# Expert results weighted on leaving PSUM and added by the scatter into two sums per token

## The chip, the cores and the metric

The kernel runs on one core of one Trainium2 chip. The metric is device time in microseconds (us) of one launch. The kernel before takes 664.97 us, the median of three runs (664.3 to 666.75).

## The reference, cut to what matters

A layer of 2048 tokens by 256 features: a retention block with its own MLP, then a mixture of experts. The change touches the second half alone, from the expert outputs to the sum over experts. All arithmetic is float32.

```python
x = hidden_states.reshape(-1, H)                      # 2048 x 256
routing_probs = softmax(x @ gate_w.T)                 # 16 experts
topk_w, topk_idx = top_k(routing_probs, 4)
topk_w = topk_w / topk_w.sum(-1)
combine = (one_hot(topk_idx, 16) * topk_w[..., None]).sum(1)
shared = silu_mul(x @ shared_gate_up.T) @ shared_down.T * sigmoid(x @ shared_gate_vec.T)
for each expert e:
    h = silu_mul(x @ w_gu[e].T)                       # 176 hidden features
    sparse += (h @ w_d[e].T) * combine[:, e]
out = x_in + gb * (shared + sparse)
```

## The kernel before, in words

One program per engine, ordered by hand-placed semaphores; nothing is planned by costs. Two blocks follow each other with a barrier between them.

**First block.** Retention over 16 tiles of 128 tokens, then the first MLP over 4 groups of 512 tokens. SP (the DMA-issuing engine) works down one list. After the retention loads it issues 20 DMAs at L1077 that fill the DRAM table `dispatched` (80 tiles of 128 rows, 260 floats a row) from a zeroed tile `fill`; column 256 of each such row holds a spare destination number. Then SP waits for the last tile of retention (`x2_lo`), and only behind that wait do the loads of the shared expert's weights (L1066) and the next `x` tiles stand.

**Second block, shared stage.** The shared expert's MLP runs over 4 groups g of 6 blocks b. VectorE (DVE) carries between its blocks the routing work, placed by `route(g, b)`: `bases` and `slots(k)` (where each token's k-th choice goes in `dispatched`), `less_best` (logits minus their maximum), `weigh(k)` (the exponential of the k-th choice, by L1661 and L1662), `share` (the normalized weights). ScalarE (ACT) takes the exponentials (L1554, L1555) in block g = 0, b = 5, between two Silu activations. GpSimd (POOL) writes the destination number of the k-th choice (token x 4 + k) into column 256 of the token rows (`number`, L1527) and scatters the rows into `dispatched`, 64 indirect DMAs (L1542), paced by the gate products of TensorE (PE).

**Second block, expert stage.** 80 tiles of 128 dispatched rows, each of one expert. SP loads a tile into one of 16 buffers `xe` (L1869); PE transposes it (L2009), multiplies by the gate and up weights (L2025), transposes the hidden features (L2035) and multiplies by the down weights (L2043, L2045); ACT and DVE split each operand into a high and a low part. `result` on DVE (L1972) multiplies the PSUM result by the vector `gb` into one of 4 buffers `yb`, and `send` on POOL (L1893) scatters the 128 rows by an indirect DMA to the DRAM table `results`, one row per token and choice. `alone` is an instruction that does nothing, ahead of each scatter. `send(j)` waits for `y` of tile j only. `result(j)` waits until the scatter of tile j - 4 has landed, and the load of tile j until that of tile j - 16 has.

**Second block, last stage.** When all 80 scatters have landed, SP loads for each of 16 token tiles its four rows per token (L1884, 512 KB each). DVE forms `acc = ys[k] * weights[k] + acc` for k = 0 to 3, starting from the residual rows, tiles in pairs: 64 operations (L1990). ACT issues the store of a finished tile (L1940).

Of the kernel before, what the change touches and what calls it, by code (L numbers as in the profile page):

```python
# [16 lines left out]
ALU = mybir.AluOpType  # L17
# [3 lines left out]
P = 128  # L21
N = 2048
# [30 lines left out]
def shape_tables():  # L53
# [27 lines left out]
        "t_tiles": np.ascontiguousarray(np.broadcast_to(np.arange(ETILES, dtype=f32)[None], (P, ETILES))),  # L81
        "t_dest": ((np.arange(NT)[None, None, :] * P + s[:, None, None]) * TOPK + np.arange(TOPK)[None, :, None]).astype(np.int32),
        "t_spare": (SPARE + np.arange(4)[None, :] * P + s[:, None]).astype(np.int32),
    }
# [27 lines left out]
def mlp_buffers(sb):  # L112

    b1, b2 = sb("b1", [P, FB]), sb("b2", [P, E])
    wr = sb("wr", [P, KB, NR])
    xt, res = sb("xt2", [P, TPG, E]), sb("res", [P, TPG, E])
    stats = sb("m_st6", [P, 2, 6]), sb("m_mv", [P, 2, 2]), sb("m_ve", [P, 2, 1]), sb("m_rstd", [P, 2, 1])
    xn, hT32 = sb("m_xn", [P, 2, E]), sb("hT32", [P, 2, KB, P])
    fill, spare = sb("fill", [P, 4, ROW]), sb("spare", [P, 4], mybir.dt.int32)
    return b1, b2, wr, xt, res, stats, xn, hT32, fill, spare  # L120


def build(nc, io, out):
    ctx = ExitStack()
    dram = {n: nc.dram_tensor(n, shape, F32, kind="Internal").ap() for n, shape in (
        ("dispatched", (ETILES * P, ROW)), ("results", (N * TOPK + 4 * P, E)), ("x3_rows", (N, E)), ("x4_rows", (N, E)))}
    with ctx:
# [895 lines left out]
def mlp(nc, io, sem, wait, alone, bank, ident, neghalf, modb, h_all, x2T, wf1, wf2, act1, a1, near, early, h3T,  # L1023
# [9 lines left out]
    stage = rows[:, STAGE:NT, :].rearrange("p t c -> p (t c)")[:, 0:2 * KB * GU].rearrange("p (c k n) -> p c k n", c=2, k=KB)  # L1033
    names = """st_in0 st_in1 w_hi w_lo zeros spare_in fill gab xb b1in b2in wr_in x_in0 x_in1 x_in2 x_in3 res1 res f_ps act a_hi a_lo fc2 x3
        st6 mv ve rstd xn h3 tr_ps h32 hi lo lg_ps lg versus ahead order chosen start before
# [16 lines left out]
    def sync(sp):  # L1052
# [41 lines left out]
        for i in range(TPG):  # L1094
            store(NT - TPG + i, i)
        sp.wait_ge(s_filled, 16 * (ETILES // 4))
        sp.wait_ge(S["x3_out"], 16 * NT)
        for i in range(TPG):
            sp.wait_ge(S[f"row_out{i}"], 16 * NG)

    def load_spare():
        nc.sync.dma_start(spare[:, :], io["t_spare"]).then_inc(S["spare_in"], 16)

    def empty_rows():
        pool = nc.gpsimd
        nc.gpsimd.memset(fill[:, :, :], 0.0).then_inc(S["zeros"], 1)
        pool.wait_ge(S["zeros"], 1)
        pool.wait_ge(S["spare_in"], 16)
        nc.gpsimd.tensor_copy(fill[:, :, E:E + 1].bitcast(mybir.dt.int32), spare[:, :].unsqueeze(2)).then_inc(S["fill"], 1)

# [291 lines left out]
def shared_and_dispatch(nc, io, sb, sem, wait, alone, bank, gb, weights, tile_expert, h3T, rows, logits,  # L1402
# [16 lines left out]
    steps, tile_no = sb("steps", [P, NX]), sb("tile_no", [P, ETILES])  # L1419
    dest = sb("dest", [P, TOPK, NT], INT)  # L1420
    best = sb("best", [P, NT])
# [5 lines left out]
    ecount = sb("ecount", [1, ETILES])  # L1427
    wsum, wrec = sb("wsum", [P, NT]), sb("wrec", [P, NT])
    names = """tab_in ones st_in0 st_in1 w_hi w_lo z_ps g_ps u_ps act hid a_hi a_lo fc2 x_in0 x_in1 x_in2 x_in3 sh x4 x4_out0 x4_out1 x4_out2 x4_out3
# [84 lines left out]
    def gpsimd(pool):  # L1514
        nc.gpsimd.memset(rows[:, :, E:ROW], 0.0).then_inc(S["pad"], 1)
        nc.gpsimd.memset(ones[:, :], 1.0).then_inc(S["ones"], 1)
# [30 lines left out]
    def scalar(act):  # L1547
# [39 lines left out]
    def vector(dve):  # L1587
# [71 lines left out]
        def weigh(k):  # L1659

            chain(nc.vector.scalar_tensor_tensor(flat(pick), flat(order), float(k), flat(ez), ALU.is_equal, ALU.mult))  # L1661
            chain(nc.vector.tensor_reduce(weights[:, k, :], pick[:, :, :], AX.X, ALU.add))  # L1662

        def share():

            chain(nc.vector.tensor_reduce(wsum[:, :], weights[:, :, :].rearrange("p k t -> p t k"), AX.X, ALU.add))
            chain(nc.vector.reciprocal(wrec[:, :], wsum[:, :]))
            nc.vector.tensor_tensor(weights[:, :, :], weights[:, :, :], wrec[:, :].unsqueeze(1).broadcast_to([P, TOPK, NT]), ALU.mult).then_inc(S["weighed"], 1)

# [131 lines left out]
def experts_and_combine(nc, io, sem, wait, alone, bank, ident, gb, weights, tile_expert, wgu, rows, dram, s_down, out, home, before):  # L1801
# [84 lines left out]
    def gpsimd(pool):  # L1886
        pool.wait_ge(before["weighed"], 1)
# [12 lines left out]
        for r in range(YR):  # L1900
            pool.wait_ge(s_sent[r], 16 * ETILES // YR)

    def scalar(act):
# [34 lines left out]
        for t in range(NT):  # L1938
            act.wait_ge(s_sum[TOPK - 1], t + 1)
            act.dma_start(out_tiles[t, :, :], acc[:, t, :]).then_inc(s_out, 16)  # L1940
        act.wait_ge(s_out, 16 * NT)

    def vector(dve):
# [40 lines left out]

        def add(t, k):
            if k == 0:
                dve.wait_ge(s_ys[t], 16)
            else:
                dve.wait_ge(s_sum[k - 1], t + 1)
            nc.vector.scalar_tensor_tensor(acc[:, t, :], ys[t][:, k, :], weights[:, k, t:t + 1],  # L1990
                                           rows[:, t, 0:E] if k == 0 else acc[:, t, :], ALU.mult, ALU.add).then_inc(s_sum[k], 1)
# [102 lines left out]
```

## Time and profile before

| | |
|---|---|
| median of three runs | 664.97 us |
| the profiled execution, its own time | 666.45 us |
| its span in the trace | 664.3 us |
| PE busy | 550.3 us (83%) |
| DVE busy | 480.5 us (72%) |
| ACT busy | 285.6 us (43%) |
| POOL busy | 323.4 us (49%) |
| DMA packets, bytes | 66298, 92.42 MB |
| HBM read, written | 53.82 MB, 35.95 MB |
| mean granted TensorE clock | 0.92 of full speed |

Busy time is that of instructions which compute (or, on POOL, issue an indirect DMA); shares are of the span. The execution's own time is 2.15 us longer than the span, by what lies around it. The shared stage runs from about 331 to 453 us of the span, the expert stage from there to 632, the last stage to the end.

### The profile page before, as it was taken

Reading aid. Unit: us, or ns where it says so; the run is one execution under the profiler, and the core shown is the slowest. Engines: PE = TensorE matmul, PEld = TensorE weight load, DVE = VectorE, ACT = ScalarE, POOL = GpSimd, SP = SyncE. Lnnn points to the kernel's source line nnn. Section 1 sums busy time; section 2 is a strip of 40 time slices with the busy share of each in tenths; the row PEclk is TensorE's granted clock in tenths of the full one; section 3 lists DMA queues with packets and bytes.
Section 4 is the critical chain, followed back from the end, with each engine's and each line's share of the span. In section 5 each row is a group of like instructions: output and inputs, shape, how many; then the busy total and the mean of one; then the engine's idle time right before and its main releaser. Section 6 shows DMA issues by size and latency. Waiting matters only on the chain.

```text
span 664.3 us, 14436 instructions
## 1 busy us (share of the span) xinstructions
PE 550.3 (83%) x4154; PEld 480.5 (72%) x4155; DVE 480.5 (72%) x1194; ACT 285.6 (43%) x696; POOL 323.4 (49%) x391
## 2 busy tenths in 40 slices
PE   2668889889898899998489979896999999999700
PEld 0357677777776788987368768685999999999600
DVE  1377978878774379898667787656677677777568
ACT  2323644454554665544135434434444444444300
POOL 1235567767665637445117777730344444444500
PEclk8788989999999999999589989996899999999955
DMA  9311212121499052111127666876644444443187
GB/s 316 135 41 41 73 50 62 58 79 39 138 315 300 2 151 74 56 49 63 56 65 224 206 187 178 252 221 224 200 130 137 119 129 131 125 124 103 71 344 296
DMA packets 66298, 92.42 MB, mean 139 GB/s; under 512 B 8528, under 2 KB 55504, under 8 KB 66256
## 3 DMA queue, kind: packets, MB, share of 16 engines
q1 hardware_dynamic: 56048, 69.86, 35.3%
q0 software_dynamic: 6912, 19.01, 7.7%
q10 hardware_dynamic: 3296, 3.03, 1.4%
q8 instruction: 22, 0.36, 0.2%
q14 instruction: 20, 0.16, 0.1%
HBM read 53.82 MB, written 35.95 MB: 135 GB/s over the span
## 4 chain that ended last, share of the span: by engine, by line
PE 31%; DVE 10%; issue 3%; ACT 3%; DMA 3%; SPq 0%; POOL 0%; DVEq 0%; ACTq 0%; POOLq 0%
PE bank L2025 12%; PE bank L2043 4%; PE bank L1764 4%; DVE wda_lo L1990 4%; PE bank L1780 3%; PE bank L2045 3%; PE bank L2009 3%; PE bank L2035 3%; ACT s_a_hi L1571 1%; DVE hid L1681 1%; DVE s_a_lo L1687 1%; DMA stage<-shared_d 1%; DMA stage<-expert_gu 1%; DMA wgu_hi<-results 1%; DVE sh L1697 1%
## 5 line engine op out<-in xcount | busy, mean ns | idle before, releaser
L1893 POOL DMA_INDIRECT results<-yb,xe x80 | 76.7, 959 | 111.0 <-DVE yb L1972 107.4
L1542 POOL DMA_INDIRECT dispatched<-rows,slot x64 | 67.9, 1060 | 34.6 <-issue 14.9
L2025 PE MATMUL bank<-wgu_hi,xT_hi 128*128 x160 | 60.7, 379 | 5.3 <-DVE xT_lo L1953 5.3
L1966 DVE TENSOR_TENSOR e_hT_lo<-bank,e_hT_hi 128x256 fp32r<-128x256 f32 x80 | 34.0, 425 | 33.5 <-ACT e_hT_hi L1926 33.4
L2025 PE MATMUL bank<-wgu_lo,xT_hi 128*128 x160 | 53.2, 332 | 0.0
L2025 PE MATMUL bank<-wgu_hi,xT_lo 128*128 x160 | 53.0, 332 | 0.0
L699 DVE TENSOR_TENSOR probs<-bank,causal 128x512 f32<-128x512 f32 x64 | 42.2, 684 | 10.0 <-PE bank L872 10.0
L1926 ACT CAST e_hT_hi<-bank 128x256 fp32r<-128x256 f32 x80 | 29.9, 373 | 41.2 <-PE bank L2035 41.1
L1921 ACT ACTIVATE e_sg<-bank 128x176 f32<-128x176 f32 x80 | 25.4, 318 | 51.5 <-PE bank L2025 51.5
L570 POOL TENSOR_TENSOR orms<-omse,neghalf 128x16 f32<-128x16 f32 x16 | 46.7, 2919 | 1.7 <-POOL omse L567 0.8
L1764 PE MATMUL bank<-h3T_hi,wsg_hi 128*128 128x512 f32 x88 | 36.9, 420 | 6.1 <-ACT hid L1568 2.1
L1196 DVE TENSOR_TENSOR a_lo<-act,a_hi 128x512 fp32r<-128x512 f32 x32 | 25.6, 800 | 16.2 <-ACT a_hi L1167 16.1
L2025 PEld LDWEIGHTS bank<-wgu_hi,xT_hi 128*128 128x128 f32 x160 | 31.4, 196 | 8.1 <-issue 6.3
L1352 PE MATMUL bank<-wf_hi,a_hi 128*128 128x256 f32 x128 | 36.4, 284 | 0.9 <-DVE a_lo L1196 0.8
L1571 ACT CAST s_a_hi<-hid 128x512 fp32r<-128x512 f32 (+1 forms) x24 | 14.9, 620 | 51.7 <-DVE hid L1681 44.8
L1352 PE MATMUL bank<-wf_hi,a_lo 128*128 128x256 f32 x128 | 36.1, 282 | 0.0
L1352 PE MATMUL bank<-wf_lo,a_hi 128*128 128x256 f32 x128 | 36.1, 282 | 0.0
L1764 PE MATMUL bank<-h3T_lo,wsg_hi 128*128 128x512 f32 x88 | 35.8, 407 | 0.0
L1764 PE MATMUL bank<-h3T_hi,wsg_lo 128*128 128x512 f32 x88 | 35.5, 403 | 0.0
L1780 PE MATMUL bank<-wsd_hi,s_a_hi 128*128 128x256 f32 x96 | 29.6, 308 | 5.0 <-DVE wsd_lo L1590 2.5
L1972 DVE TENSOR_TENSOR yb<-bank,gb 128x256 f32<-128x256 f32 x80 | 33.2, 415 | 0.7 <-PE bank L2045 0.7
L562 POOL TENSOR_TENSOR qk<-rot,rot 128x512 f32<-128x512 f32 x16 | 20.5, 1278 | 26.8 <-DVE rot L693 26.8
(234 smaller groups left out, 1872.3 us busy)
## 6 DMA issues: line engine op xcount, KB each, us to landing
dispatched<-fill SPq DMA_DIRECT2D x20, 520.0 KB, 10.0
xe<-dispatched SPq DMA_DIRECT2D x80, 130.0 KB, 2.3
trig<-t_trig SPq DMA_DIRECT2D x16, 512.0 KB, 3.7
stage<-expert_gu SPq DMA_DIRECT2D x16, 352.0 KB, 3.5
wgu_hi<-results SPq DMA_DIRECT2D x11, 512.0 KB, 8.3
xt<-L_attn_x SPq DMA_DIRECT2D x32, 128.0 KB, 2.8
wgu_lo<-results SPq DMA_DIRECT2D x5, 512.0 KB, 16.6
x_rows<-h_all SPq DMA_DIRECT2D x16, 128.0 KB, 2.0
```

Source lines behind the costliest of these rows:

```text
L570: nc.gpsimd.tensor_tensor(orms[:, :], omse[:, :], neghalf[:, :], ALU.pow).then_inc(S["orms"], 1)
L699: nc.vector.tensor_tensor(probs[:, 4 * b:4 * b + 4, :], b_s[b][:, :].rearrange("p (h s) -> p h s", s=P), causal[:, :].unsqueeze(1).broadca ...
L1352: mm = nc.tensor.matmul(dst, a1[an][:, b % RING, cols], wf2[wn][:, b, :], start=(b == 0 and j == 0 and i % 2 == 0), stop=(b == FB - 1 and ...
L1542: pool.indirect_dma_start(out=dram["dispatched"], out_offset=bass.IndirectOffsetOnAxis(ap=slot[:, k, t:t + 1], axis=0), in_=rows[:, t, :], ...
L1764: mm = nc.tensor.matmul(dst[b % 2][:, :], wsg[wn][:, k, start:start + P], h3T[xn_][:, k, cols], start=(k == 0 and i == 0), stop=(k == KB - ...
L1780: mm = nc.tensor.matmul(dst, a1[an][0:m, b % RING, i * P:i * P + P], wsd[wn][0:m, b, :], start=(b == 0 and an + wn == 0 and i % 2 == 0), s ...
L1893: pool.indirect_dma_start(out=dram["results"], out_offset=bass.IndirectOffsetOnAxis(ap=xe[r][:, E:E + 1].bitcast(INT), axis=0), in_=yb[:, ...
L1926: nc.scalar.copy(hT[0][:, q, :], hT_bank[p][:, 0:2 * P]).then_inc(S["h_hi"], 1)
L1966: nc.vector.tensor_tensor(hT[1][:, q, :], hT_bank[p][:, 0:2 * P], hT[0][:, q, :].bitcast(F32), ALU.subtract).then_inc(S["h_lo"], 1)
L1972: nc.vector.tensor_tensor(yb[:, r % YR, :], y_bank[r % 2][:, 0:E], gb[:, :], ALU.mult).then_inc(S["y"], 1)
L1990: nc.vector.scalar_tensor_tensor(acc[:, t, :], ys[t][:, k, :], weights[:, k, t:t + 1], rows[:, t, 0:E] if k == 0 else acc[:, t, :], ALU.mu ...
L2025: mm = nc.tensor.matmul(gu_bank[p][:, 0:GU], xT[xn_][:, p, k, :], wgu[wn][:, k, e, :], start=(k == 0 and i == 0), stop=(k == KB - 1 and i ...
```

## The change

1. A table `sums` with two rows per token replaces `results` with four. Columns 256 and 257 of a dispatched row hold the two destination numbers (token x 2, token x 2 + 1), the same for all choices; column 258 holds the weight of this choice: 1.0 for the first, `weights[k]` = exp(logit - best logit) for the others.
2. `sums` has to start at zero: 10 more DMAs of 512 KB follow the 20 fills on SP.
3. `number(0)` copies the two destination columns; `number(k)` for k = 1 to 3 waits until the k-th weight is there and copies it.
4. `less_best` moves on DVE from block g = 0, b = 4 to b = 0; the exponentials on ACT from b = 5 to b = 2; `weigh(1)`, `weigh(2)` to g = 0, b = 4 and 5, `weigh(3)` to g = 1, b = 0, `weigh(0)` to g = 1, b = 5. `share` ends with the reciprocal of the sum of the four weights, in `weights[:, 0]`.
5. `result` multiplies by the weight column and by `gb` in one operation. The scatter of tile j adds to row side j mod 2 (`compute_op=ADD`), and `send(j)` waits in addition until the scatter of tile j - 2 has landed.
6. The last stage loads two rows per token (256 KB a tile). DVE adds them (`both`) and forms `acc = sum * weights[0] + rows` (`add`): 32 operations.

```diff
+ZEROED = (N + 4 * P) * 2 // (4 * P)
+        sums_zero = dram["sums"].rearrange("(m r p) e -> m p r e", r=4, p=P)
+        for n in range(ZEROED):
+            sp.dma_start(sums_zero[n, :, :, :], fill[:, :, 0:E]).then_inc(S["zeroed"], 16)
...
-            nc.gpsimd.tensor_copy(rows[:, cols, E:E + 1].bitcast(INT), dest[:, k, cols].unsqueeze(2)).then_inc(S["col"], 1)
+            if k == 0:
+                nc.gpsimd.tensor_copy(rows[:, cols, E:E + SUMS].bitcast(INT), dest[:, cols, :]).then_inc(S["col"], 1)
+            else:
+                pool.wait_ge(S["weighed"], k)
+                nc.gpsimd.tensor_copy(rows[:, cols, E + SUMS:E + SUMS + 1], weights[:, k, cols].unsqueeze(2)).then_inc(S["col"], 1)
...
-                if isinstance(g, int) and g == 0 and b == NB - 1:
+                if isinstance(g, int) and g == 0 and b == 2:
                     exponentials()
...
         def weigh(k):
 
+            if k == 1:
+                dve.wait_ge(S["exps"], 1)
             chain(nc.vector.scalar_tensor_tensor(flat(pick), flat(order), float(k), flat(ez), ALU.is_equal, ALU.mult))
...
                 slots(0)
                 low_down(0)
+                less_best()
...
-            elif g == 0 and b == 4:
-                less_best()
+            elif g == 0:
+                weigh(b - 3)
             elif g == 1 and b == 0:
+                weigh(3)
                 shared_gate()
             elif g == 1 and b < 5:
                 experts_of_tiles(b - 1)
-                weigh(b - 1)
             elif g == 1:
+                weigh(0)
                 share()
...
         def send(j, r):
+            side = r % SUMS
             pool.wait_ge(S["y"], per(1, j))
+            wait(pool, s_sent[(r - SUMS) % YR], sent(j - SUMS, (r - SUMS) % XR))
             alone(pool)
-            pool.indirect_dma_start(out=dram["results"], out_offset=bass.IndirectOffsetOnAxis(ap=xe[r][:, E:E + 1].bitcast(INT), axis=0),
-                                    in_=yb[:, r % YR, :], in_offset=None).then_inc(s_sent[r % YR], 16)
+            pool.indirect_dma_start(out=dram["sums"], out_offset=bass.IndirectOffsetOnAxis(ap=xe[r][:, E + side:E + side + 1].bitcast(INT), axis=0),
+                                    in_=yb[:, r % YR, :], in_offset=None, compute_op=ALU.add).then_inc(s_sent[r % YR], 16)
...
-            nc.vector.tensor_tensor(yb[:, r % YR, :], y_bank[r % 2][:, 0:E], gb[:, :], ALU.mult).then_inc(S["y"], 1)
+            nc.vector.scalar_tensor_tensor(yb[:, r % YR, :], y_bank[r % 2][:, 0:E], xe[r][:, E + SUMS:E + SUMS + 1], gb[:, :],
+                                           ALU.mult, ALU.mult).then_inc(S["y"], 1)
...
-        for t in range(0, NT, 2):
-            for k in range(TOPK):
-                add(t, k)
-                add(t + 1, k)
+        def both(t):
+            dve.wait_ge(s_ys[t], 16)
+            nc.vector.tensor_tensor(ys[t][:, 0, :], ys[t][:, 0, :], ys[t][:, 1, :], ALU.add).then_inc(s_sum[0], 1)
+
+        def add(t):
+            dve.wait_ge(s_sum[0], t + 1)
+            nc.vector.scalar_tensor_tensor(acc[:, t, :], ys[t][:, 0, :], weights[:, 0, t:t + 1], rows[:, t, 0:E], ALU.mult, ALU.add).then_inc(s_sum[1], 1)
+
+        both(0)
+        for t in range(NT):
+            if t + 1 < NT:
+                both(t + 1)
+            add(t)
```

## Rows read from the trace of the kernel before

**Rows 1.** The page's costliest groups: busy us, mean ns, idle before, releaser.

```profile
L1893 POOL DMA_INDIRECT results<-yb,xe x80 | 76.7, 959 | 111.0 <-DVE yb L1972 107.4
```

**Rows 2.** Busy time by window (PE, PEld, DVE, ACT, POOL, clock, DMA share, GB/s), expert stage.

```profile
560.00:600.00 40.00, 39.90 (x291) 38.58 (x291) 29.49 (x97) 18.69 (x58) 18.22 (x19) 1.00 0.43 127
```

**Rows 3.** Timeline, POOL and DVE in the expert stage: start, us, engine, line.

```profile
469.26 0.96 POOL L1893 DMA_INDIRECT results<-yb,xe  x1 [26.25 <-DVE yb L1972]
478.07 0.96 POOL L1893 DMA_INDIRECT results<-yb,xe  x1 [1.05 <-DVE yb L1972]
480.08 0.96 POOL L1893 DMA_INDIRECT results<-yb,xe  x1 [1.05 <-DVE yb L1972]
563.69 0.41 DVE L1972 TENSOR_TENSOR yb<-bank,gb 128x256 f32<-128x256 f32 x1
564.86 0.96 POOL L1893 DMA_INDIRECT results<-yb,xe  x1 [1.19 <-DVE yb L1972]
```

**Rows 4.** Instructions of L1893: time from a scatter's start to its landing.

```profile
DMA to landing us min/median/max: 2.4/2.9/5.0
```

**Rows 5.** The same of L1869 (loads of `xe`), then of the stores of `out`.

```profile
DMA to landing us min/median/max: 2.0/2.3/9.2
DMA to landing us min/median/max: 1.7/6.1/7.7
```

**Rows 6.** Busy time by window, the last scatters alone on the DMA engines.

```profile
630.00:632.00 2.00, 0.00 (x0) 0.00 (x0) 0.00 (x0) 0.00 (x0) 0.77 (x1) 0.50 0.37 131
```

**Rows 7.** Timeline, the end of the expert stage.

```profile
624.24 0.96 POOL L1893 DMA_INDIRECT results<-yb,xe  x1 [1.03 <-DVE yb L1972]
627.23 0.42 DVE L1972 TENSOR_TENSOR yb<-bank,gb 128x256 f32<-128x256 f32 x1 [0.40 <-PE bank L2045]
629.81 0.96 POOL L1893 DMA_INDIRECT results<-yb,xe  x1 [0.30 <-issue]
```

**Rows 8.** The chain that ended last, its end: start, us, what.

```profile
629.81 2.40 DMA results<-yb,xe
632.68 4.29 DMA wgu_hi<-results
637.00 24.63 DVE wda_lo L1990 x62
```

**Rows 9.** Last stage: a window, a group of L1990 (ns), SP's issues.

```profile
634.00:658.00 24.00, 0.00 (x0) 0.00 (x0) 21.49 (x55) 0.00 (x0) 0.00 (x0) 0.50 1.02 403
L1990 DVE SCALAR_TENSOR_TENSOR wda_lo<-wgu_hi,weights,wda_lo x33: 479/480/480, 637.4 to 654.8; 128x256 f32<-128x256 f32 x33
632.30 5.24 SPq L1884 DMA_DIRECT2D wgu_hi<-results  x11
```

**Rows 10.** SP's issues in the first block, and the window behind the fills.

```profile
179.75 29.03 SPq L1077 DMA_DIRECT2D dispatched<-fill  x20
233.11 0.90 SPq L1066 DMA_DIRECT2D rows<-shared_gu  x2
216.00:232.00 16.00, 14.27 (x97) 12.69 (x95) 5.96 (x9) 9.97 (x20) 10.96 (x14) 1.00 0.01 2
```

**Rows 11.** Instructions of L1697: three-operand DVE operation out of PSUM, in ns.

```profile
L1697 DVE SCALAR_TENSOR_TENSOR sh<-bank,sgate,gb x16: 472/477/484, 376.4 to 451.8; 128x256 f32<-128x256 f32 x16
```

**Rows 12.** Timeline of the shared stage, ACT, DVE and POOL.

```profile
348.60 0.62 ACT L1550 CAST wsd_hi<-stage 128x512 fp32r<-128x512 f32 x1 [1.44 <-DMA stage<-shared_d]
349.25 0.69 DVE L1590 TENSOR_TENSOR wsd_lo<-stage,wsd_hi 128x512 fp32r<-128x512 f32 x1 [0.74 <-ACT wsd_hi L1550]
354.68 0.68 DVE L1681 TENSOR_TENSOR hid<-hid,bank 128x512 f32<-128x512 f32 x1
360.43 0.41 DVE L1640 TENSOR_REDUCE best<-logits 128x16 f32<-128x256 f32 x1
361.22 0.88 DVE L1590 TENSOR_TENSOR wgu_lo<-stage,wgu_hi 128x704 fp32r<-128x704 f32 x1
363.50 1.28 ACT L1554 ACT_TABLE_LOAD   x1
366.02 1.28 ACT L1568 ACT_TABLE_LOAD   x1
367.76 0.21 POOL L1527 COPY rows<-dest 128x8 int32<-128x8 int32 x1
374.66 0.43 DVE L1661 SCALAR_TENSOR_TENSOR pick<-order,chosen 128x256 f32<-128x256 f32 x1
375.58 0.89 DVE L1590 TENSOR_TENSOR wgu_lo<-stage,wgu_hi 128x704 fp32r<-128x704 f32 x1
```

More of the change, by code:

```diff
@@ L43 @@
 ETILES = N * TOPK // P + NX
+ZEROED = (N + 4 * P) * 2 // (4 * P)
 ROW = E + 4
-SPARE = N * TOPK
+SUMS = 2
 G = 512
@@ L81, in shape_tables @@
         "t_tiles": np.ascontiguousarray(np.broadcast_to(np.arange(ETILES, dtype=f32)[None], (P, ETILES))),
-        "t_dest": ((np.arange(NT)[None, None, :] * P + s[:, None, None]) * TOPK + np.arange(TOPK)[None, :, None]).astype(np.int32),
-        "t_spare": (SPARE + np.arange(4)[None, :] * P + s[:, None]).astype(np.int32),
+        "t_dest": ((np.arange(NT)[None, :, None] * P + s[:, None, None]) * SUMS + np.arange(SUMS)[None, None, :]).astype(np.int32),
+        "t_spare": ((N + np.arange(4)[None, :, None] * P + s[:, None, None]) * SUMS + np.arange(SUMS)[None, None, :]).astype(np.int32),
     }
@@ L118, in mlp_buffers @@
     xn, hT32 = sb("m_xn", [P, 2, E]), sb("hT32", [P, 2, KB, P])
-    fill, spare = sb("fill", [P, 4, ROW]), sb("spare", [P, 4], mybir.dt.int32)
+    fill, spare = sb("fill", [P, 4, ROW]), sb("spare", [P, 4, SUMS], mybir.dt.int32)
     return b1, b2, wr, xt, res, stats, xn, hT32, fill, spare
@@ L125, in build @@
     dram = {n: nc.dram_tensor(n, shape, F32, kind="Internal").ap() for n, shape in (
-        ("dispatched", (ETILES * P, ROW)), ("results", (N * TOPK + 4 * P, E)), ("x3_rows", (N, E)), ("x4_rows", (N, E)))}
+        ("dispatched", (ETILES * P, ROW)), ("sums", ((N + 4 * P) * SUMS, E)), ("x3_rows", (N, E)), ("x4_rows", (N, E)))}
     with ctx:
@@ L1033, in mlp @@
     stage = rows[:, STAGE:NT, :].rearrange("p t c -> p (t c)")[:, 0:2 * KB * GU].rearrange("p (c k n) -> p c k n", c=2, k=KB)
-    names = """st_in0 st_in1 w_hi w_lo zeros spare_in fill gab xb b1in b2in wr_in x_in0 x_in1 x_in2 x_in3 res1 res f_ps act a_hi a_lo fc2 x3
+    names = """st_in0 st_in1 w_hi w_lo zeros zeroed spare_in fill gab xb b1in b2in wr_in x_in0 x_in1 x_in2 x_in3 res1 res f_ps act a_hi a_lo fc2 x3
         st6 mv ve rstd xn h3 tr_ps h32 hi lo lg_ps lg versus ahead order chosen start before
@@ L1096, in sync @@
         sp.wait_ge(s_filled, 16 * (ETILES // 4))
+        sp.wait_ge(S["zeroed"], 16 * ZEROED)
         sp.wait_ge(S["x3_out"], 16 * NT)
@@ L1101, in load_spare @@
     def load_spare():
-        nc.sync.dma_start(spare[:, :], io["t_spare"]).then_inc(S["spare_in"], 16)
+        nc.sync.dma_start(spare[:, :, :], io["t_spare"]).then_inc(S["spare_in"], 16)
     def empty_rows():
@@ L1108, in empty_rows @@
         pool.wait_ge(S["spare_in"], 16)
-        nc.gpsimd.tensor_copy(fill[:, :, E:E + 1].bitcast(mybir.dt.int32), spare[:, :].unsqueeze(2)).then_inc(S["fill"], 1)
+        nc.gpsimd.tensor_copy(fill[:, :, E:E + SUMS].bitcast(mybir.dt.int32), spare[:, :, :]).then_inc(S["fill"], 1)
     def gate_bias():
@@ L1419, in shared_and_dispatch @@
     steps, tile_no = sb("steps", [P, NX]), sb("tile_no", [P, ETILES])
-    dest = sb("dest", [P, TOPK, NT], INT)
+    dest = sb("dest", [P, NT, SUMS], INT)
     best = sb("best", [P, NT])
@@ L1427, in shared_and_dispatch @@
     ecount = sb("ecount", [1, ETILES])
-    wsum, wrec = sb("wsum", [P, NT]), sb("wrec", [P, NT])
+    wsum = sb("wsum", [P, NT])
     names = """tab_in ones st_in0 st_in1 w_hi w_lo z_ps g_ps u_ps act hid a_hi a_lo fc2 x_in0 x_in1 x_in2 x_in3 sh x4 x4_out0 x4_out1 x4_out2 x4_out3
@@ L1514, in gpsimd @@
     def gpsimd(pool):
-        nc.gpsimd.memset(rows[:, :, E:ROW], 0.0).then_inc(S["pad"], 1)
+        nc.gpsimd.memset(rows[:, :, E + SUMS:ROW], 1.0).then_inc(S["pad"], 1)
         nc.gpsimd.memset(ones[:, :], 1.0).then_inc(S["ones"], 1)
@@ L1659, in weigh @@
         def weigh(k):
+            if k == 1:
+                dve.wait_ge(S["exps"], 1)
             chain(nc.vector.scalar_tensor_tensor(flat(pick), flat(order), float(k), flat(ez), ALU.is_equal, ALU.mult))
-            chain(nc.vector.tensor_reduce(weights[:, k, :], pick[:, :, :], AX.X, ALU.add))
+            nc.vector.tensor_reduce(weights[:, k, :], pick[:, :, :], AX.X, ALU.add).then_inc(S["weighed"], 1)
+            dve.wait_ge(S["weighed"], (1, 2, 3, 0).index(k) + 1)
         def share():
             chain(nc.vector.tensor_reduce(wsum[:, :], weights[:, :, :].rearrange("p k t -> p t k"), AX.X, ALU.add))
-            chain(nc.vector.reciprocal(wrec[:, :], wsum[:, :]))
-            nc.vector.tensor_tensor(weights[:, :, :], weights[:, :, :], wrec[:, :].unsqueeze(1).broadcast_to([P, TOPK, NT]), ALU.mult).then_inc(S["weighed"], 1)
+            nc.vector.reciprocal(weights[:, 0, :], wsum[:, :]).then_inc(S["weighed"], 1)
         def low_down(n):
@@ L1829, in experts_and_combine @@
     s_ys = [sem(f"c_ys{t}") for t in range(NT)]
-    s_sum = [sem(f"c_sum{k}") for k in range(TOPK)]
+    s_sum = [sem(f"c_sum{k}") for k in range(SUMS)]
     s_out = sem("c_out")
     flat = [w[:, :, :, :].rearrange("p k e n -> p (k e n)").bitcast(F32) for w in wgu]
-    TILES_IN = KB * NX * GU // (TOPK * E)
-    ys = [flat[t // TILES_IN][:, (t % TILES_IN) * TOPK * E:(t % TILES_IN + 1) * TOPK * E].rearrange("p (k e) -> p k e", e=E) for t in range(NT)]
+    TILES_IN = KB * NX * GU // (SUMS * E)
+    ys = [flat[t // TILES_IN][:, (t % TILES_IN) * SUMS * E:(t % TILES_IN + 1) * SUMS * E].rearrange("p (k e) -> p k e", e=E) for t in range(NT)]
     acc = wda[1][:, :, :].bitcast(F32)
-    res = dram["results"][0:N * TOPK, :].rearrange("(t p k) e -> t p k e", k=TOPK, p=P)
+    res = dram["sums"][0:N * SUMS, :].rearrange("(t p k) e -> t p k e", k=SUMS, p=P)
     out_tiles = out.rearrange("a (t p) e -> (a t) p e", p=P)
@@ L1886, in gpsimd @@
     def gpsimd(pool):
-        pool.wait_ge(before["weighed"], 1)
+        pool.wait_ge(before["weighed"], TOPK + 1)
         nc.gpsimd.memset(hx[:, :, :], 0.0).then_inc(S["zero"], 1)
         def send(j, r):
+            side = r % SUMS
             pool.wait_ge(S["y"], per(1, j))
+            wait(pool, s_sent[(r - SUMS) % YR], sent(j - SUMS, (r - SUMS) % XR))
             alone(pool)
-            pool.indirect_dma_start(out=dram["results"], out_offset=bass.IndirectOffsetOnAxis(ap=xe[r][:, E:E + 1].bitcast(INT), axis=0),
-                                    in_=yb[:, r % YR, :], in_offset=None).then_inc(s_sent[r % YR], 16)
+            pool.indirect_dma_start(out=dram["sums"], out_offset=bass.IndirectOffsetOnAxis(ap=xe[r][:, E + side:E + side + 1].bitcast(INT), axis=0),
+                                    in_=yb[:, r % YR, :], in_offset=None, compute_op=ALU.add).then_inc(s_sent[r % YR], 16)
         def body(j, r, live):
@@ L1909, in high_w @@
             nc.scalar.copy(dst, st).then_inc(S["w_hi"], 1)
-        act.wait_ge(before["weighed"], 1)
+        act.wait_ge(before["weighed"], TOPK + 1)
         def high_x(j, p):
@@ L1938, in scalar @@
         for t in range(NT):
-            act.wait_ge(s_sum[TOPK - 1], t + 1)
+            act.wait_ge(s_sum[1], t + 1)
             act.dma_start(out_tiles[t, :, :], acc[:, t, :]).then_inc(s_out, 16)
@@ L1983, in vector @@
         pipeline(nc.vector, body)
[L1985 to L1991, printed above, removed]
-        dve.wait_ge(S["x4_in"], 16)
-        for t in range(0, NT, 2):
-            for k in range(TOPK):
-                add(t, k)
-                add(t + 1, k)
+        def both(t):
[4 more added lines that the diff above has]
+            nc.vector.scalar_tensor_tensor(acc[:, t, :], ys[t][:, 0, :], weights[:, 0, t:t + 1], rows[:, t, 0:E], ALU.mult, ALU.add).then_inc(s_sum[1], 1)
+        dve.wait_ge(S["x4_in"], 16)
+        both(0)
[3 more added lines that the diff above has]
+            add(t)
     def tensor(pe):
```

## The prediction

> **What bounds the kernel now.** I read the costliest groups first, then windows of the expert stage, the timeline of POOL, the times to landing, and the end of the chain of waits. The reader is to see four things.
>
> First, the expert stage belongs to PE: 39.9 of 40 us busy at full clock, DVE 29.5, POOL 18.2, DMA share 0.43 [rows 2]. A scatter starts every 2.01 us (480.08 - 478.07) and sits idle for a result between two [rows 1, 3]. Over the stage the pace is a little slower: 469.26 to 624.24 is 75 tiles, 2.066 us each [rows 3, 7].
>
> Second, a scatter has a long way. It takes 2.9 us from its start to its landing in the median, 2.4 when nothing else moves [rows 4, 8]. And POOL wakes slowly: the result ends at 563.69 + 0.41 = 564.10, the scatter released by it starts at 564.86, 0.76 us later [rows 3].
>
> Third, the last results are ready early (627.65) but the last scatter starts at 629.81: POOL issues its last ones back to back [rows 7].
>
> Fourth, the last stage is bound twice over. From 637.00 DVE runs 62 operations in 24.63 us, 0.397 each at pitch (480 ns each, overlapping), and in the same time DMA is full: share 1.02, 403 GB/s [rows 8, 9]. From the last landing (632.21) to the end of the span (664.3) are 32.1 us.
>
> **The last stage, halved.** Loads fall from 8.39 to 4.19 MB, stores stay at 2.10 MB, DVE operations fall from 64 to 32. By DVE: first tile some 3.6 us behind the last landing (before: 4.8 to the first ready pair, now a smaller load), 32 x 0.397 = 12.7, then the last store 2.6 (1.7 for the quickest, with its issue and the end) [rows 5, 8, 9]: 18.9. By DMA: it starts to move 1.8 us behind the last landing; 6.29 MB at 403 GB/s is 15.6, less the last store, plus the last pair of operations and that store: 19 to 19.9, should rows of 2 KB for 4 KB cost some rate [rows 9]. SP issues 16 loads at 0.48 each, 7.6 us, faster than they move [rows 9]. I take 19.9. Gain 32.1 - 19.9 = **12.2 us**; ends 9 and 13.
>
> **The result on DVE.** The operation out of PSUM goes from 415 to 477 ns, by the like one [rows 11]; 80 of them lie beside PE (DVE at 29.5 of 40, some 31 after) [rows 2]. Cost 0. Without that cover: 5 us.
>
> **The zeroing.** 20 fills are issued in 29.03 us, so they drain at 1.45 us each; ten more take 14.5 and SP is at its wait by 223.3, ten us before it is released at 233.11. The DMA engines had nothing in 216 to 232 [rows 10]; 5.24 MB at the fills' rate, some 0.3 MB per us, is 16.6 to 17.8 us and ends at 232.7 to 234. Cost 0, at most 1 us on the loads at 233.11. Nothing else is queued on SP in between.
>
> **The shared stage.** `less_best` in b = 0 takes 0.79 us (360.43 to 361.22) ahead of a DVE operation that waits for ACT at 348.60 anyway [rows 12]; hidden. The exponentials with their two table loads (1.28 each, some 3.1 us in all) move from b = 5 to b = 2; there DVE is not back at `hid` before 354.68, where ACT had it ready 1.3 us earlier, so about 2.2 us come in, and about 1.9 go at b = 5 (2.8, less a `weigh` of 0.92, 374.66 to 375.58, that now stands there) [rows 12]. In g = 1, where DVE sets the pace, three of four `weigh` leave (2.8 us), one comes to b = 0 (0.9). POOL copied the second choice's column at 367.76; `weigh(1)` should be ready by 362.5 and each later one a block ahead, so the added wait on POOL costs nothing, and nobody queues behind it [rows 12]. Sum: 1 us gained, ends -1.5 and +2.5.
>
> **The accumulating scatter, the disputed term.** No row shows one. What decides is a chain of its own: scatter j starts, lands, POOL wakes, scatter j + 2 starts. Call its length L. Two tiles of PE's work last 4.0 to 4.13 us. With a plain scatter L would be 2.9 + 0.76 = 3.66 [rows 3, 4]: the new wait alone is free in the middle. Behind it on POOL stand only further scatters; for them wait DVE (four buffers), then PE (two PSUM banks) and SP's loads (16 buffers), so with L beyond 4.13 the whole stage goes at L / 2 per tile: 39.5 us more for each us of L, and 1 more at the last landing.
>
> What adding costs, D = L - 3.66, from both sides: the lower end is 0 (a shorter trip is excluded, it is the same trip and a read more), the upper end is a whole further read of 128 rows from HBM, 2.0 us [rows 5]. Between them the nearest rows are a load's quickest landing, 2.0, against a store's, 1.7 (reading from HBM rather than SBUF: 0.3), and the DMA share of a scatter: two scatters (131 GB/s x 2 us = 262 KB) in 0.37 x 2 us, 0.37 each, of which a second read should add something under the whole [rows 5, 6]. That is 0.3 to 0.67. I take **0.5**, the middle of these: L = 4.16.
>
> The Trainium skill, "DMA: Bandwidth & Descriptors", in "Rules for kernel authors", says an accumulating DMA reads its destination and writes later with nothing holding the bytes in between, so a second one on the same rows must wait for the first; it is why this wait cannot be dropped, and the trace of before has no such transfer to test it. Its section "Anatomy of one DMA" makes a transfer a fixed 2.0 us plus bytes over 436 GB/s; doubling the 131 KB read would by that add 0.3, an estimate from the page, and give L = 3.96, wholly hidden, the second rival below. Against the change speaks "Collectives: The Full Stack", "The bandwidth ceiling": an adding transfer issues two source reads and moves at half a copy's rate, which doubles the 0.37 us above: an estimated D of 0.37 from that alone, L = 4.03.
>
> The end: the last start is the later of 469.26 + 39.5 L and about 632.2 (with L = 4.0 the sends at 622.24 and 624.24 carry the last four in steps of 2 per side, to 632.24 instead of 629.81) [rows 3, 7]. With L = 4.16: 633.6. Landing 3.4 later: 637.0, against 632.2: **cost 4.8 us**.
>
> **Sum.** 637.0 + 19.9 - 1.0 = 655.9 of span, with 2.15 around it 658.0 against the profiled execution's 666.45: 8.4 less. The median of the runs shown lies 1.5 below that execution, so 656.6; I say **657**.
>
> **Rivals.**
> 1. *The adding scatter becomes the bound* (slower). Same chain, D larger, because the read goes ahead of each write or POOL's own 0.96 us grows with the work of describing it. The span is 487.4 + 40.5 L, and equals that of before at L = 4.37, D = 0.71. That is its point. At D = 1.0 (L = 4.66) it is 676, time 677; at D = 1.5, 697. For it: the slack is only 0.35 to 0.47 us and the term is multiplied by 40. Against: the median of 2.9 holds waits for other transfers that a paced chain may avoid.
> 2. *Adding is hidden* (D up to 0.47): the last start stays at 632.2, span about 654, and with the full gains of the other stages 651 to 655.
> 3. *The last stage doesn't halve*: short rows at the 300 GB/s of the fills make 6.3 MB take 21 us, and the gain 7 instead of 12: time 662. Against: loads and stores together now hold 403 GB/s with stores of 1 KB rows [rows 9].
> 4. *The change doesn't do what it says*: the weights come late and stall the dispatch on POOL. Each us would count once at most; 658 to 660. The margin of 5 us at the first of them [rows 12] speaks against it.
>
> **How the numbers follow.** The forecast (D from 0.47 to 0.63) 0.25, rival 2 0.27, rival 3 or 4 0.06, rival 1 0.42, of which D between 0.63 and 0.79, where gain and cost meet within 0.5% (3.3 us, about what a measurement of this kernel can tell from no change), 0.12 and beyond 0.30. The single likeliest band is the short one at and just above the hidden point, on which forecast and rival 2 agree within 4 us; hence 657. Faster 0.57, same 0.12, slower 0.31. The range must reach far up, since 40 us hang on each us of D: 651 to 683 (D about 1.15) leaves out 2 in 10, most of it above. Of the faster cases alone the range is 651 to 661.
>
> **What the profile after would show.** Pace of scatters in the expert stage: 2.0 to 2.1 us, PE still 39 of 40 busy, if the forecast holds; if rival 1, POOL's idle time is released by its own earlier scatter, and PE falls under 38 of 40. The time from start to landing, 3.4 in the median. The last scatter's start near 633. 32 operations in some 13 to 16 us behind it. SP at its wait before 233. The exponentials around 353, and no idle time of POOL ahead of the weight copies. The prediction is wrong if the landing takes over 3.6 us or the last stage more than 22.

## The result: 3.1% slower, and the profile after

The changed kernel takes 685.8 us (median; 685.23 to 686.92), the kernel before beside it 665.66 (664.3 to 666.75): ratio 1.0306, 95% interval 1.028 to 1.0331. The forecast was 657, its range 651 to 683. The profiled execution has a span of 683.7 us, 19.4 more than before.

First the costliest groups of the page after (busy us, mean ns, idle before and its releaser).

```profile
L1908 POOL DMA_INDIRECT sums<-yb,xe x80 | 124.6, 1558 | 95.3 <-DVE yb L1987 77.7
L1987 DVE SCALAR_TENSOR_TENSOR yb<-bank,xe,gb 128x256 f32<-128x256 f32 x80 | 38.5, 481 | 43.6 <-DMA sums<-yb,xe 41.9
```

The scatter takes 1558 ns of POOL for 959 [rows 1], and DVE, which wrote its results without waiting before, now waits 41.9 us for scatters to land: its four buffers are full. Next the chain of waits after, its shares of the span.

```profile
DMA 28%; DVE 9%; PE 5%; issue 5%; ACT 3%; SPq 2%; DVEq 0%; POOLq 0%; ACTq 0%
DMA sums<-yb,xe 25%; PE bank L1777 2%; PE bank L1793 1%; ACT s_a_hi L1580 1%; DMA wgu_hi<-sums 1%; DVE hid L1692 1%; SPq L1897 1%; DVE yb L1987 1%; DVE s_a_lo L1698 1%; DMA stage<-shared_d 1%; DVE sh L1708 1%; PE bank L2042 1%; DVE ecount L1658 1%; DMA stage<-expert_d 1%; DVE wgu_lo L1599 1%
```

A quarter of the span is now the way of one scatter after another; before, the chain ran through PE, and its shares on the page of before were these:

```profile
PE 31%; DVE 10%; issue 3%; ACT 3%; DMA 3%; SPq 0%; POOL 0%; DVEq 0%; ACTq 0%; POOLq 0%
```

In the same window as [rows 2] PE has work for 35.0 of 40 us (POOL 25.7, DMA share 0.68 at fewer GB/s); columns as there.

```profile
560.00:600.00 40.00, 35.02 (x243) 32.80 (x244) 26.62 (x86) 15.86 (x50) 25.68 (x17) 1.00 0.68 109
```

The timeline of POOL near the end of the stage, and then the time from start to landing of all 80 scatters (L1908), answer to [rows 3, 4].

```profile
628.24 1.55 POOL L1908 DMA_INDIRECT sums<-yb,xe  x1 [1.22 <-DVE yb L1987]
630.10 1.56 POOL L1908 DMA_INDIRECT sums<-yb,xe  x1 [0.30 <-issue]
632.77 1.55 POOL L1908 DMA_INDIRECT sums<-yb,xe  x1 [1.11 <-DVE yb L1987]
634.62 1.56 POOL L1908 DMA_INDIRECT sums<-yb,xe  x1 [0.30 <-DVE yb L1987]
637.27 1.55 POOL L1908 DMA_INDIRECT sums<-yb,xe  x1 [1.08 <-DVE yb L1987]
```

```profile
DMA to landing us min/median/max: 3.6/3.8/6.0
```

Two scatters go out back to back (1.86 apart), then POOL waits for the first of them. The one of 632.77 lands at 636.55, the next of its side starts at 637.27, 0.72 later: the distance of two tiles is landing plus waking (the time from the landing until POOL starts the next). Read scatter by scatter, the way to the landing is 3.99 us in the mean, the time from a landing to the next start of the same side 0.89, together 4.88. In 42 of 78 cases the latter is 0.72 to 0.76 and never less; where it is longer, up to 1.9, the start mostly stands 1.86 behind the other side's scatter, for which POOL was still busy. The profile puts such waits down to `yb`, written by DVE at about the same moment, since DVE waits for the same landing. But that operation writes the result of a later tile; of the two waits ahead of a scatter the one named is not the one that held it. From 500 to 620 us starts of one side are 4.9 us apart in the mean, at the stage's end, with the loads of `xe` over, 4.5.

The end of the chain after, and the last stage, answer to [rows 8, 9].

```profile
659.56 3.69 DMA sums<-yb,xe
671.55 8.29 DMA wgu_hi<-sums
```

```profile
664.00:680.00 16.00, 0.00 (x0) 0.00 (x0) 11.57 (x30) 0.00 (x0) 0.00 (x0) 0.50 1.00 341
L2003 DVE TENSOR_TENSOR wgu_hi<-wgu_hi x16: 417/424/426, 666.0 to 679.9; 128x256 f32<-128x256 f32 x16
```

And SP's list after, as in [rows 10].

```profile
208.30 15.16 SPq L1081 DMA_DIRECT2D sums<-fill  x10
232.68 0.89 SPq L1067 DMA_DIRECT2D rows<-shared_gu  x2
```

The account of the two spans: the first scatter starts at 466.48 for 469.26 (-2.8); from the first to the last start 193.1 for 160.55 (+32.5, 2.444 us a tile); the last one takes 3.7 to land for 2.4 (+1.3); from there to the end 20.4 for 32.1 (-11.7). Sum +19.3 of 19.4.

### The profile page after: what moved, and what is told of

The parts are those of the page before. It is cut to its first block, busy times and chain, and to the rows that moved or that the text cites. A ratio compares the mean times of both kernels' runs of the same rounds, so it can differ in the third digit from the quotient of the medians.

```text
span 683.7 us, 14435 instructions
## 1 busy us (share of the span) xinstructions
PE 555.9 (81%) x4154; PEld 478.5 (70%) x4155; DVE 470.8 (69%) x1161; ACT 284.8 (42%) x696; POOL 370.7 (54%) x391
## 3 DMA queue, kind: packets, MB, share of 16 engines
q0 software_dynamic: 14592, 19.01, 16.4%
## 4 chain that ended last, share of the span: by engine, by line
DMA 28%; DVE 9%; PE 5%; issue 5%; ACT 3%; SPq 2%; DVEq 0%; POOLq 0%; ACTq 0%
DMA sums<-yb,xe 25%; PE bank L1777 2%; PE bank L1793 1%; ACT s_a_hi L1580 1%; DMA wgu_hi<-sums 1%; DVE hid L1692 1%; SPq L1897 1%; DVE yb L1987 1%; DVE s_a_lo L1698 1%; DMA stage<-shared_d 1%; DVE sh L1708 1%; PE bank L2042 1%; DVE ecount L1658 1%; DMA stage<-expert_d 1%; DVE wgu_lo L1599 1%
## 5 line engine op out<-in xcount | busy, mean ns | idle before, releaser
L1908 POOL DMA_INDIRECT sums<-yb,xe x80 | 124.6, 1558 | 95.3 <-DVE yb L1987 77.7
L1551 POOL DMA_INDIRECT dispatched<-rows,slot x64 | 66.0, 1031 | 34.4 <-issue 15.2
L1987 DVE SCALAR_TENSOR_TENSOR yb<-bank,xe,gb 128x256 f32<-128x256 f32 x80 | 38.5, 481 | 43.6 <-DMA sums<-yb,xe 41.9
L1981 DVE TENSOR_TENSOR e_hT_lo<-bank,e_hT_hi 128x256 fp32r<-128x256 f32 x80 | 33.7, 421 | 19.3 <-ACT e_hT_hi L1941 19.3
L563 POOL TENSOR_TENSOR qk<-rot,rot 128x512 f32<-128x512 f32 x16 | 20.4, 1278 | 25.8 <-DVE rot L694 25.8
L1968 DVE TENSOR_TENSOR xT_lo<-bank,xT_hi 128x256 fp32r<-128x256 f32 x80 | 33.0, 414 | 0.2
```

The costliest lines, as they stand in the source:

```text
L1551: pool.indirect_dma_start(out=dram["dispatched"], out_offset=bass.IndirectOffsetOnAxis(ap=slot[:, k, t:t + 1], axis=0), in_=rows[:, t, :], ...
L1908: pool.indirect_dma_start(out=dram["sums"], out_offset=bass.IndirectOffsetOnAxis(ap=xe[r][:, E + side:E + side + 1].bitcast(INT), axis=0), ...
L1968: nc.vector.tensor_tensor(xT[1][:, p, :, :].rearrange("p k s -> p (k s)"), t_bank[p][:, 0:E], xT[0][:, p, :, :].bitcast(F32).rearrange("p ...
L1981: nc.vector.tensor_tensor(hT[1][:, q, :], hT_bank[p][:, 0:2 * P], hT[0][:, q, :].bitcast(F32), ALU.subtract).then_inc(S["h_lo"], 1)
L1987: nc.vector.scalar_tensor_tensor(yb[:, r % YR, :], y_bank[r % 2][:, 0:E], xe[r][:, E + SUMS:E + SUMS + 1], gb[:, :], ALU.mult, ALU.mult).t ...
```

## The experiments

Each is an edit of the changed kernel unless it says otherwise. The groups ran on different chips, on which the kernel before took 665 to 670 us, so the ratio to it is what compares. The expected times do not know how fast the chip is; where it matters, the ratio times 665.7 (the kernel before beside the changed one in the result) stands beside the measured time, as that of the first chip.

**1. Is it the wait or the adding?** Copy instead of add, the wait kept.

```diff
-                                    in_=yb[:, r % YR, :], in_offset=None, compute_op=ALU.add).then_inc(s_sent[r % YR], 16)
+                                    in_=yb[:, r % YR, :], in_offset=None).then_inc(s_sent[r % YR], 16)
```

> The changed kernel with its wait for the scatter of tile j - 2 and all else, but the scatter copies and doesn't add (so of the tiles that meet in a row only the last is in the sums). Theory A, the adding transfer is the cost: a scatter takes 0.96 us on POOL again, lands 2.9 us after its start, the next one of the same side can start 3.7 us after it, under the 4.1 us of two tiles on PE; the stage runs at 2.03 to 2.07 us per tile, time 650 to 654 us. Theory B, the new wait alone is the cost, by the 0.7 us in which POOL wakes: pace stays near 2.44, time 680 or more.

655.61 us against 669.82, ratio 0.9796 (0.9773 to 0.982), or 652 on the first chip. The page of this kernel:

```profile
L1908 POOL DMA_INDIRECT sums<-yb,xe x80 | 76.7, 959 | 109.0 <-DVE yb L1987 57.7
```

From the first start, 468.3, to the last, 629.0, the pace is 2.034 us a tile (79 steps), for 2.032 before. The new wait alone costs nothing to speak of; it is the adding that lengthens the chain past two tiles of PE. Without the adding the change gains 2%.

**2. Adding without the wait.** Tiles j mod 4 = 2, 3 add to a table of their own.

```diff
-            wait(pool, s_sent[(r - SUMS) % YR], sent(j - SUMS, (r - SUMS) % XR))
-            pool.indirect_dma_start(out=dram["sums"], ...
+            pool.indirect_dma_start(out=dram["sums" if r % 4 < 2 else "sums_b"], ...
```

> The changed kernel, where the scatters of every second pair of tiles add to a table of their own (which is neither zeroed nor read, so their part is missing from the output), and send(j) waits for no earlier scatter; tiles of one row side are four apart, which the four result buffers keep in order. All scatters still add. Theory A, the chain over two tiles (start, landing, waking) sets the pace: without it the stage returns to PE's 2.03 to 2.1 us per tile, POOL being free every 1.86; time 653 to 657 us. Theory C, the adding scatters are too much work for POOL (1.56 us each) or the DMA engines (1.1 us each beside the loads): pace stays above 2.3, time above 674.

655.91 us, ratio 0.9801 (0.9781 to 0.982). The window and POOL's timeline:

```profile
560.00:600.00 40.00, 40.00 (x301) 39.76 (x299) 31.39 (x100) 19.20 (x60) 30.88 (x20) 1.00 0.79 129
```

```profile
618.02 1.55 POOL L1907 DMA_INDIRECT sums<-yb,xe  x1 [0.45 <-issue]
620.02 1.56 POOL L1907 DMA_INDIRECT sums_b<-yb,xe  x1 [0.44 <-issue]
```

All 80 scatters add, each takes 1.56 us of POOL, and PE is back at 40.0 of 40. Neither POOL nor the DMA engines (share 0.79) are the bound: theory C falls, the chain over two tiles stands. With 1 it says that the loss needs both, the adding and the wait at a distance of two.

**3. All tiles on one side.** `side = 0`, and the wait is for tile j - 1.

> The changed kernel with all tiles on row side 0, each scatter waiting for the one before it. The output is complete. Theory A: pace is the whole chain for each tile, 4.3 to 4.9 us in place of 2.44, the stage 150 to 195 us longer: time 835 to 880. If a part of the chain of two tiles was work that shares engines and not latency, less: under 820.

855.49 us against 669.64, ratio 1.2782 (1.2751 to 1.2813), as theory A has it. 468.0 to 829.5 is 4.576 us a tile: the whole chain, landing 3.8 (median of this kernel) and the rest, 0.76, from a landing to the next start. POOL's timeline shows it one by one:

```profile
666.10 1.55 POOL L1908 DMA_INDIRECT sums<-yb,xe  x1 [2.92 <-issue]
670.60 1.56 POOL L1908 DMA_INDIRECT sums<-yb,xe  x1 [2.94 <-DVE yb L1987]
675.10 1.55 POOL L1908 DMA_INDIRECT sums<-yb,xe  x1 [2.95 <-DVE yb L1987]
```

```profile
L1908 POOL DMA_INDIRECT sums<-yb,xe x80: 1554/1558/1610, 468.0 to 829.5; - x80
DMA to landing us min/median/max: 3.6/3.8/5.7
```

Over two sides a pair takes 4.89, 0.31 more than this single chain: so much comes with the second side (later starts behind POOL's other scatter, and landings of 3.99 for 3.82 in the mean), the rest is the chain's own length.

**4. One side adds, the other copies.** `compute_op=ALU.add if side == 0 else ALU.bypass`.

> The changed kernel, where tiles of row side 1 copy and only those of side 0 add (so of side 1 the last tile's result alone counts). Both waits stay. Theory A (a side's own chain of start, landing, waking): side 0 is as slow as before the edit, a pair of tiles takes 4.5 us or more, time 670 to 684. Rival, that the adding scatters hinder each other (POOL's turns, DMA engines): half of the excess goes, a pair takes under 4.3, time under 665.

677.92 us, ratio 1.0138 (1.0099 to 1.0178). The scatters, all 80:

```profile
L1908 POOL DMA_INDIRECT sums<-yb,xe x80: 971/1278/1611, 470.4 to 654.0; - x80
```

That is 2.324 us a tile, 4.65 a pair. The adding side's own chain, 4.58 in 3, holds both sides, as theory A has it, and the rival's 4.3 is far off; the neighbour's adding is worth the 0.24 between 4.65 and 4.89.

**5. What the adding costs by: bytes or rows.** 64 of 256 columns to a table of short rows.

```diff
-            pool.indirect_dma_start(out=dram["sums"], ...
-                                    in_=yb[:, r % YR, :], ...
+            pool.indirect_dma_start(out=dram["short"], ...
+                                    in_=yb[:, r % YR, 0:E // 4], ...
```

> The changed kernel, where each adding scatter carries 64 of the 256 columns (256 bytes a row) to a table of its own that isn't read, so the expert part is missing from the output; rows, waits and number of transfers are the same. Theory bytes (the second read and the add cost by size): the trip behind POOL's 1.56 us falls by half or more, start to landing under 3.2 us, the pace returns to 2.1, time 652 to 660. Theory rows (each of 128 rows costs its own read, add and write, whatever its length): start to landing stays over 3.5, pace over 2.3, time above 675.

661.8 us, ratio 0.9885 (0.9858 to 0.9913), or 658 on the first chip. The group, the last scatter on its way in the chain, and the queue of the scatters:

```profile
L1908 POOL DMA_INDIRECT short<-yb,xe x80 | 124.6, 1557 | 67.0 <-DVE yb L1987 51.2
```

```profile
636.06 3.15 DMA short<-yb,xe
q0 software_dynamic: 14592, 11.15, 10.0%
```

POOL's time does not move with the bytes (1557 ns), and the number of packets does not either. The trace of this kernel has no landings of the scatters but that of the last one: 3.15 us for the 3.69 of the changed kernel's last one. So with a quarter of the bytes the way behind POOL is 1.59 us for 2.13, a quarter shorter and not by half or more, as theory bytes had it. With the 0.72 of waking the chain is then some 3.87 us (an estimate from this one scatter), just under the 4.0 of two tiles of PE, and the pace, from 470.2 to 636.1, is 2.10. Theory bytes has the pace and the time right and the size of the effect wrong; theory rows, pace over 2.3, falls.

**6. The order of the routing work alone**, on the kernel before: `less_best` in block 0, the exponentials in block 2, the weights from block 4 on.

> The kernel before with nothing changed but the order of routing work in the shared stage (logits minus maximum in block 0, exponentials in block 2, weights from block 4 of the first group on). If the 2.8 us by which the first scatter of the changed kernel starts earlier come from this order: 662 to 664 us against 665.5. If they come from elsewhere (the shorter share, the row layout): 665 to 667.

667.08 us against 669.82, ratio 0.9971 (0.9945 to 0.9997), or 663.7 on the first chip, which would be the first alternative. Still it is inconclusive as to the 2.8 us: the interval nearly touches 1, and in this kernel's profile the stretch from PE's first product of the second block (332.55) to the first scatter (471.30) is 138.8 us, against 137.6 before (331.64 to 469.26) and 135.5 after. In 1 to 5, all with the changed kernel's shared stage, the first scatter starts anywhere from 468.0 to 470.4. What the order gives is at most a few tenths of a per cent.

**7. Three sums a token.** If the chain of 4.9 us is the bound, a distance of three tiles (6 us) hides it. In a loop of 16 tiles three sides cannot go strictly round, so the first version has one irregular place, by which scatters wait at a distance of two or four instead of three in four places of 16.

```diff
-SUMS = 2
+SUMS = 3
+    SIDES = [r % 3 for r in range(XR - 1)] + [1]
+    APART = [next(d for d in range(1, XR) if SIDES[(r - d) % XR] == SIDES[r]) for r in range(XR)]
...
+            if apart < YR:
+                wait(pool, s_sent[(r - apart) % YR], sent(j - apart, (r - apart) % XR))
```

> Three sums per token in place of two: sides in the order 0, 1, 2 with one irregular place in 16 tiles, so that a scatter waits for one three tiles before it (in two places of 16, two before it, in two, four). 15 zeroing transfers for 10, three rows per token loaded at the end, 48 DVE operations there. The output is complete. Theory A: a chain of 4.9 us spans 6.2 us of PE's work, so the stage runs at 2.03 to 2.1 per tile; the last stage gives back 5 to 6 of its 12 us; time 657 to 662, under both kernels. Theory C: above 676.

667.98 us against 669.82, ratio 0.9968 (0.9948 to 0.9987): under the kernel before, but short of the figure (663.5 on the first chip, for 657 to 662). SP's list and POOL's first instruction of the second block say why.

```profile
208.93 22.88 SPq L1081 DMA_DIRECT2D sums<-fill  x15
233.45 1.68 SPq L1067 DMA_DIRECT2D rows<-shared_gu  x2
335.84 0.13 POOL L1520 MEMSET rows<- 128x16 f32 x1 [8.00 <-POOLq L147]
```

The load of the shared weights at 233.45 takes 1.68 us to issue for 0.89, and the second block starts at 335.8 instead of 331.0: the fifteen zeroing transfers seem to be still moving when the weights are due. 8 tests it.

**8. The same with 6 of the 15 behind the stores of the second and third group of the first MLP.** The text expected of 9 says third and fourth, but the edit puts them behind those of the second and third; SP issues them at 281.9 and 307.9.

> Three sums in a loop over 16 tiles, with 6 of the 15 zeroing transfers behind the stores of the first MLP; only this differs from the first kernel with three sums. If the 4.8 us by which that one's second block began late come from 15 transfers in one go: ratio to the kernel before 0.989 to 0.992 against 0.9968. If the later place only moves the delay: no change.

662.33 us against 666.92, ratio 0.9934 (0.9913 to 0.9954). The second block starts at 332.0. Most of the delay was the fifteen transfers in one go; of its 3.9 us the ratios show 2.3 in the time. The figure hoped for (0.992) lies within the interval.

**9. The expert stage written out for 80 tiles**, sides strictly in turn, zeroing spread as in 8.

```diff
-        with eng.Fori(1, ETILES // XR) as j:
-            for r in range(XR):
-                body(j * XR + r, r, lambda lag: True)
+        for t in range(XR, ETILES):
+            body(t, t % XR, lambda lag: True)
```

> Three sums per token, sides strictly in turn, which needs the expert stage written out for its 80 tiles instead of a loop over 16; 9 of the 15 zeroing transfers stay where they are, 6 go behind the stores of the third and fourth group of the first MLP, where the DMA engines are 17% busy. The output is complete. Against three sums in a loop (668.0 against 669.8): the second block starts 4 to 5 us earlier, POOL is no longer held by the irregular places; time 1% to 1.5% under the kernel before. If fetching the longer code costs, no gain over the loop.

660.55 us against 669.64, ratio 0.9867 (0.9833 to 0.9901). How much of it is owed to writing out? The kernel before with it (and with the order of 6):

> The kernel before with the early order of the routing work and the expert stage written out for its 80 tiles; plain scatters to four rows a token, nothing zeroed. It tells how much of the 1.3% of the written-out kernel with three sums is owed to neither sums nor adding. If the three sums carry it: 0.3 to 0.6% under the kernel before, 3 to 6 us over the three sums. If writing out does: 1% or more under.

661.68 us against 666.92, ratio 0.9938 (0.9915 to 0.9961). The two once more, both on one chip:

> The written-out kernel with three sums, beside the next one on the same chip. If the three sums gain by themselves: ratio to the kernel before 0.985 to 0.989, below the next one's beyond the intervals. If not: both near 0.992.

> The written-out kernel before with the early routing order and four plain rows. Ratio 0.992 to 0.996 if the three sums gain by themselves; equal to the other one if not.

Three adding sums: 657.16 us, ratio 0.9867 (0.9843 to 0.9891). Four plain rows: 660.36, ratio 0.9926 (0.9902 to 0.9949). The intervals don't meet. The ends of these two chains, first four rows, then three sums:

```profile
623.65 2.41 DMA results<-yb,xe
630.92 24.63 DVE wda_lo L1993 x62
```

```profile
625.21 3.78 DMA sums<-yb,xe
637.26 13.25 DMA wgu_lo<-sums
```

From the last landing to the end of the span four rows take 32.1 us (626.1 to 658.2), three sums 26.1 (629.0 to 655.1). Of these 6 us the scatters give 3.7 back: the last one lands 1.4 us later after its start, and from the first to the last start three sums take 158.5 us for 156.2. Of that, 1.7 us fall in the last 15 tiles, where four rows run at 1.84 us a tile and three sums at 1.95; POOL needs 1.86 us for each adding scatter and 1.26 for each plain one. Three adding sums in a written-out stage beat both kernels of this case, by 1.3% against the one before; writing out and the early order carry 0.7 of it (not told apart), the sums 0.6.

## Why the prediction was wrong, by its own steps

**The step that failed is the size of D**, what adding costs one scatter. The forecast took 0.5, the middle of 0.3 for reading from HBM and that plus 0.37 for a second read on the DMA engines, and nothing for POOL. What the sum left out is POOL's own instruction: 0.60 us more (1558 ns for 959), in every link of the chain. Rival 1 named it and gave it no number. The way behind POOL's instruction grew by 0.3 in the median (3.8 - 1.56 = 2.24 for 2.9 - 0.96 = 1.94) and by 0.7 in the last scatter, with the loads of `xe` over (3.69 - 1.56 = 2.13 for 2.40 - 0.96 = 1.44): the two ends of the forecast's 0.3 to 0.67. Together that is 0.9 by the medians, as by the single chain of 3 (4.58 - 3.66 = 0.92), and 1.3 by the last scatter. With the 0.31 that the second side adds to the single chain, a term that the forecast did not have, D is 1.23; that is what the pace says (4.89 - 3.66) and 2.5 times the 0.5. Had POOL's time stayed, a D of 0.3 would have been hidden by the forecast's own rule, at a span of 654; this is an estimate that leaves the second side's 0.31 out, and no run tests it.

**The mechanism was right.** The chain over two tiles, named as the disputed term, sets the pace. One side gave 4.576 a tile, four apart gave PE's pace (2, 3), and the plain scatter with the wait kept it as well (1), which is the forecast's "the new wait alone is free". Rival 1's formula gives 487.4 + 40.5 x 4.89 = 685.4 for the span, 683.7 is what the trace shows; as 4.89 is twice the measured pace, this confirms the rest of the sum and not the chain. That the time breaks even at an L of 4.37 is borne out from its two sides alone: with some 3.87 the kernel was 1.1% faster than the one before (5), with 4.65 it was 1.4% slower (4). The forecast's own sign of being wrong, a landing over 3.6 us, came: 3.8. The chance of 0.31 for slower was low for a term multiplied by 40 with slack of 0.4, and 683 as the upper end 3 us short.

Of the two rules of the Trainium skill that the forecast set against each other, the one in "DMA: Bandwidth & Descriptors", "Anatomy of one DMA", fixed cost plus bytes, gives +0.3 where the single chain shows +0.9; it counts the making of descriptors as small, while here POOL's instruction is two thirds of the growth. That of "Collectives: The Full Stack", "The bandwidth ceiling", two source reads for one, is too low here too: the share of the scatters' queue grew from 7.7% to 16.4%, or by (16.4% of 683.7 - 7.7% of 664.3) / 80 = 0.76 us a scatter on top of 0.37, three times and not twice. That an adding transfer must wait for an earlier one on the same rows, the third thing quoted from the skill, no run here tests.

**The last stage: right.** 20.4 us for 19.9, gain 11.7 for 12.2. The rate is lower than in [rows 9], 341 GB/s for 403, with rows of 2 KB for 4 KB as the forecast feared (that the rows are the reason was not tried), and DVE waits for loads in between; the first operation starts 2.8 us behind the last landing, earlier than the 3.6 assumed.

**The result on DVE: right.** 481 ns for 415, with PE at 40.0 of 40 beside it in 2.

**The zeroing: right, and narrow.** Ten transfers are issued by 223.5, the wait ends at 232.68, the next load is issued in 0.89 us as before (0.90). 7 and 8 show the price beyond that cover, 4.8 us of later start for five more in one go.

**The shared stage.** The weights were never late: POOL's copies (L1536) stood from 366.2 on with no wait of their own. Of the gain (1 forecast, 2.8 in the profile) nothing is shown (6).

**The end of the stage.** The last scatter costs 1.3 for the forecast's 1.0 (3.4 - 2.4); its later start is contained in the pace.

## What to carry to other kernels

When a transfer must wait for an earlier one of its kind, write down the whole round (issue, landing, waking) against the distance between the two in the bound engine's time; a slack of a tenth is no slack for a term that is multiplied by the number of tiles. A change in what a transfer does can cost time on the engine that issues it as well as on its way: here 0.60 us of POOL, two thirds of the single chain's growth. If the round is too long, put the dependent transfers further apart: three sums instead of two turned 3% slower into 0.7% faster in the loop (8) and 1.3% written out (9).

## What the runs showed of the hardware

- An adding indirect DMA of 128 rows takes 1558 ns of POOL, a copying one 959. With rows of 256 bytes for 1024 the adding one takes 1557; the copying one was not tried so.
- It puts three times the packets on its queue: 14592 for 6912 in all, or, less the 48 for each of 64 dispatching scatters, 144 for 48 a scatter. With rows of 256 bytes the packets are as many, and the queue's share falls from 16.4% of 683.7 us to 10.0% of 659.7, by 0.58 us a scatter (5).

```profile
q0 software_dynamic: 14592, 19.01, 16.4%
```

- POOL starts a scatter 0.72 us at the earliest after the landing that it waited for (637.27 - 636.55), 0.76 after the end of the DVE operation that it waited for [rows 3], and 0.30 after the end of its previous one.
- Written out, the expert stage lets PE issue 302 matmuls in 40 us (the row below is of three sums, 9), and four plain rows run at (625.36 - 468.66) / 79 = 1.98 us a tile in their first run. In the loop it is 291 to 293 before, but 301 in the same window of 2, which is a loop too. What costs the loop its few matmuls was not tried.

```profile
560.00:600.00 40.00, 40.00 (x302) 40.00 (x301) 31.72 (x101) 19.29 (x61) 30.94 (x21) 1.00 0.82 134
```
